# One product for q, k and v, statistics of two tiles per instruction, and new orders of the work in an attention and FFN block

## The chip, the cores and the metric

The kernel runs on one core of a Trainium2 chip. The metric is the device time of one execution in microseconds (us), the median over several runs; lower is better.

## What is computed

The input x has 8 batches of 512 rows of 128 numbers, f32. The output is x + attention(xn) + ffn(xn), where xn is x normalised over its 128 numbers.

```python
qkv = xn @ w_qkv.T                        # 3 x 16 heads x 8
q = softmax((q . code) * scale) * scale   # 2 codes per head
k = (k . code) * scale
k_exp = exp(k - max(k over the 512 rows))
kv = cumsum(k_exp * v) / (cumsum(k_exp) + 1e-9)      # over the rows
xo = sum over codes of q * kv;  attention = xo @ w_out.T
# fp4(): blocks of 16 numbers, scaled by their maximum, rounded to an 8-value grid
h = silu(fp4(xn) @ fp4(w_gate).T) * (fp4(xn) @ fp4(w_up).T)  # 352 wide
ffn = fp4(h) @ fp4(w_down).T
```

## The kernel before, in words

All work is f32 on tiles of 128 partitions; a partition holds 4 neighbouring rows of a batch, so a batch is 4 tiles of 128x128. The weights are quantised and transposed once, at the start. The 8 batches then pass through a software pipeline: each engine runs a loop over steps, and in each step it meets a list of pieces, each for its own batch `b = step - n`. So the text order of the pieces and their `n` are the order of each engine's queue, written out by hand; the last batch has pieces of its own (`if step == ...`). Engines wait for each other on semaphores only. Pieces such as L1416 or L1481 are two throw-away products each on TensorE (30 pieces), placed in gaps of the start.

Per batch the pieces are, in the order of the data:

- Statistics: VectorE `bn_stats` per tile (4 instructions a batch, L893, L961 and others) and `bn_aggr` per tile (4, L1061, L1023 and others); ScalarE takes variance + eps and the negative mean from them; rstd and shift are made on GpSimd (GpSimd = POOL in the rows). Batches 2 and 3, and 4 to 7, share those small steps.
- `xn` on ScalarE (4 activations, L696), transposed on TensorE into the PSUM bank `t_ps` (L1757), copied out by ScalarE to `xn_t` (L794).
- v: 4 products with `wv_t` (128 columns each) into the whole bank `t_ps` (L1458), copied out to `v_sb` (L556). q and k codes: 4 products with `wqk_t` (64 columns each) into half of the bank `a_ps` (L1591). `wqk_t` is w_q and w_k times block-diagonal code matrices `code_bd`, which VectorE builds at the start (L1147, L1148).
- ScalarE takes relu of the q codes (`q_rel`, L674). VectorE takes the maximum of the k codes over the tiles (L1162), TensorE transposes it (L1692), VectorE reduces it (L1234), TensorE subtracts it in the bank (L1729, "kshift"), and ScalarE takes exp into `kv` (L786, "kexp"). Exp/ln and silu lie in two tables of ScalarE, so each batch has two table loads (L784, L629).
- GpSimd multiplies v by exp(k), one operation per code (L500, two a batch), and adds the tiles up (L337, L391, L436). TensorE sums over the partitions into `a_ps` (L1450, "base"), VectorE adds that to all (L992), sums and inverts the denominators with ScalarE's Ln and Exp (L1002, L607, L609, L1038, L1048) and makes `q_n` (L1051); GpSimd makes `o_codes` (L375); TensorE transposes and adds these into `t_ps` (L1660, L1661), and ScalarE copies out (`o_t`, L714).
- Quantising: VectorE maxima, GpSimd scalings `yx`, `xq`, `yh`, `hq` (L495, L430, L449, L516, L399, L461), ScalarE squares into the bank `s_ps`, VectorE two operations each for the grid. `xq` is transposed through `t_ps` as well (L1508, L587).
- FFN: 8 products of 352 columns (L1570, L1571, L1574, L1603, L1654, L1675, L1685, L1711), 4 silus, then 12 transposes of `hq` through `h_ps`, and 16 products for `w_out` and `w_down` into `o_ps` (L1410/L1412, L1499/L1501, L1538/L1540, L1624/L1626). VectorE adds x (L1187), SyncE stores.

A f32 product appears as two records ("x8" for four products), a transpose as one.

Of the kernel before, what the change touches and what calls it, by code (L numbers as in the profile page):

```python
# [4 lines left out]
P = 128  # L5
BATCHES, T, D = 8, 512, 128
TILES = T // P
# [4 lines left out]
FF = 352  # L12
# [19 lines left out]
DEPTH = 89  # L32


# [4 lines left out]
def block_kernel(nc, x, w_qkv, w_out_t, code_t, w_gate, w_up, w_down, out):  # L39
# [6 lines left out]
    with ExitStack() as ctx:  # L46
# [15 lines left out]
        wqk_t = sb("wqk_t", [P, 2 * HC])  # L62
        wv_t = sb("wv_t", [P, D])
# [16 lines left out]
        stats = sb("stats", [P, BATCHES, TILES, 6])  # L80
        meanvar = sb("meanvar", [P, BATCHES, TILES, 2])
# [49 lines left out]
        t_ps = bank("t_ps")  # L131
        h_ps = bank("h_ps")
        a_ps = bank("a_ps")
# [17 lines left out]
        wqkev_done = sem("wqkev_done")  # L151
# [12 lines left out]
        aggr_done = sem("aggr_done")  # L164
# [13 lines left out]
        qk_done = sem("qk_done")  # L178
        qrel_done = sem("qrel_done")
# [5 lines left out]
        v_done = sem("v_done")  # L185
# [8 lines left out]
        qsum_done = sem("qsum_done")  # L194
# [16 lines left out]
        qx_done = sem("qx_done")  # L211
        xqT_done = sem("xqT_done")
        xqt_done = sem("xqt_done")
        gate0_done = sem("gate0_done")
        silu0_done = sem("silu0_done")
        h0_done = sem("h0_done")
# [10 lines left out]
        up3_done = sem("up3_done")  # L227
# [12 lines left out]
        yhz1_done = sem("yhz1_done")  # L240
# [3 lines left out]
        hrz3_done = sem("hrz3_done")  # L244
        hqz3_done = sem("hqz3_done")
# [29 lines left out]
        pads_done = sem("pads_done")  # L275
# [19 lines left out]
        def kv_pairs(p):  # L295
            return kv[:, p, :, :].rearrange("p (a two) r -> p a two r", two=2)

# [30 lines left out]
        def _(pool):  # L328
            nc.gpsimd.memset(ident[:, :], 0.0)
            nc.gpsimd.memset(before[:, :], 1.0)  # L330
            nc.gpsimd.memset(head_of[:, :], 1.0).then_inc(filled, 1)
            for step in range(BATCHES + DEPTH):
                b = step - 52
# [4 lines left out]
                if step == 63:  # L338
                    b = BATCHES - 1
                    p = b % 2  # L340
                    pool.wait_ge(qn_done, 8)
                    nc.gpsimd.tensor_tensor(o_codes[:, p, :, :].rearrange("p j (c w) -> p j c w", w=HEAD), kv[:, p, :, 0:KV].rearrange("p j (c w) -> p j c w", w=HEAD),
                                            q_n[:, p, :, :].unsqueeze(3).broadcast_to([P, TILES, HC, HEAD]), ALU.mult).then_inc(o_done, 1)
                if step == 53:
                    nc.gpsimd.tensor_tensor(ratio[:, 4:8, :], var_eps[:, 4:8, :], guess_sq[:, 4:8, :], ALU.mult).then_inc(ratio_done, 1)
                if step == 30:
                    pool.wait_ge(fills_done, 1)
                    pool.wait_ge(vareps_done, 1)
                    nc.gpsimd.tensor_tensor(rstd[:, 0:1, :], var_eps[:, 0:1, :], minus_half[:, 0:1, :], ALU.pow).then_inc(rstd_done, 1)
                if step == 59:  # L350
                    b = BATCHES - 1
                    p = b % 2
                    pool.wait_ge(kvm_done, 8)
                    nc.gpsimd.tensor_tensor(kv[:, p, 1, :], kv[:, p, 1, :], kv[:, p, 0, :], ALU.add).then_inc(add1_done, 1)
# [1436 lines left out]
```

## Time and profile before

| | |
|---|---|
| median of 3 runs | 145.97 us (145.90 to 146.12) |
| the profiled execution | 145.66 us |
| span of its trace | 143.9 us |
| outside the span | 1.76 us |
| busy: PE, DVE, ACT, POOL | 135.2, 126.0, 115.2, 120.9 us |
| granted TensorE clock | 1.000 of full speed throughout |

PE is TensorE's products, PEld its weight loads, DVE is VectorE, ACT ScalarE, POOL GpSimd. The busy time is the time in which at least one record of the engine runs; the mean durations of records overlap a little, so what an instruction takes in its engine's queue is the distance of two starts.

### The profile page before, as it was taken

To read this page: it belongs to the slowest core of one execution; us is meant where nothing else is said; L and a number is where in the kernel's file an instruction comes from. 1 tells how busy PE (TensorE), PEld (TensorE's weight loads), DVE (VectorE), ACT (ScalarE), POOL (GpSimd) and SP (SyncE) were. 2 spreads that over 40 slices of the span, in tenths; PEclk is the share of its full clock that TensorE was granted. 3 is DMA by queue.
4 is the path that set the end of the run, shared out by engine and by line. 5 is a ranking of instruction groups with operands and counts; after the bars stand their busy time and mean duration, and the time that the engine had idled before them with its cause. 6 is when DMAs were issued, how large, how long until landed. Compare 5 with 4: busy or idle time off the path is not lost.

```text
span 143.9 us, 2675 instructions
## 1 busy us (share of the span) xinstructions
PE 135.2 (94%) x909; PEld 112.8 (78%) x909; DVE 126.0 (88%) x340; ACT 115.2 (80%) x276; POOL 120.9 (84%) x130
## 2 busy tenths in 40 slices
PE   3979999999999999999999999999999998969793
PEld 3979987598869886988698869887988685839692
DVE  0899998999899899989998999899989995999841
ACT  0376788799999989998999899989995797597450
POOL 4567688579999999999889998999599999969920
DMA  4990000000000001000100010001000200010012
GB/s 115 344 343 9 2 0 2 0 0 7 0 0 0 0 5 73 0 0 2 73 5 0 2 73 0 5 0 73 0 0 0 77 0 0 27 48 5 0 73 73
DMA packets 4078, 5.16 MB, mean 36 GB/s; under 512 B 545, under 2 KB 2145, under 8 KB 4065
## 3 DMA queue, kind: packets, MB, share of 16 engines
q1 hardware_dynamic: 3088, 4.49, 8.9%
q10 hardware_dynamic: 976, 0.51, 1.2%
q8 instruction: 7, 0.11, 0.3%
q14 instruction: 7, 0.05, 0.1%
HBM read 2.90 MB, written 2.10 MB: 35 GB/s over the span
## 4 chain that ended last, share of the span: by engine, by line
PE 75%; DVE 11%; ACT 5%; POOL 3%; DMA 2%; issue 1%
PE t_ps L1458 5%; PE a_ps L1591 4%; PE a_ps L1450 3%; PE g_ps L1603 3%; PE u_ps L1570 3%; PE g_ps L1711 3%; PE t_ps L1757 3%; PE u_ps L1574 3%; PE g_ps L1571 3%; PE o_ps L1412 3%; PE u_ps L1654 2%; PE g_ps L1675 2%; PE u_ps L1685 2%; PE o_ps L1626 2%; PE o_ps L1540 2%; PE o_ps L1501 2%
## 5 line engine op out<-in xcount | busy, mean ns | idle before, releaser
L500 POOL TENSOR_TENSOR kv<-v_sb,kv 128x512 f32<-128x512 f32 x14 | 14.8, 1077 | 0.0
L375 POOL TENSOR_TENSOR o_codes<-kv,q_n 128x1024 f32<-128x1024 f32 x7 | 13.8, 1965 | 0.1
L461 POOL TENSOR_TENSOR hq<-qh,h_max 128x704 f32<-128x704 bf16 x7 | 9.7, 1383 | 3.4 <-DVE qh L1307 3.4
L696 ACT ACTIVATE xn<-x_all,shift,rstd 128x128 f32<-128x128 f32 x28 | 11.5, 481 | 0.0
L449 POOL TENSOR_TENSOR yh<-h,h_r 128x704 f32<-128x704 f32 x7 | 9.7, 1386 | 1.5 <-ACT h_r L727 1.5
L399 POOL TENSOR_TENSOR hq<-qh,h_max 128x704 f32<-128x704 bf16 x7 | 9.7, 1386 | 0.0
L516 POOL TENSOR_TENSOR yh<-h,h_r 128x704 f32<-128x704 f32 x7 | 9.7, 1384 | 0.0
L495 POOL TENSOR_TENSOR yx<-xn,x_r 128x512 f32<-128x512 f32 x7 | 7.4, 1058 | 2.6 <-ACT x_r L811 2.6
L992 DVE TENSOR_TENSOR kv<-kv,a_ps 128x1152 f32<-128x1152 f32 x7 | 9.4, 1344 | 0.0
L629 ACT ACT_TABLE_LOAD x7 | 9.0, 1283 | 0.1
L1591 PEld LDWEIGHTS a_ps<-wqk_t,xn_t 128*128 128x128 f32 x56 | 7.3, 191 | 1.3
L784 ACT ACT_TABLE_LOAD x6 | 7.7, 1283 | 0.1
L1458 PEld LDWEIGHTS t_ps<-wv_t,xn_t 128*128 128x128 f32 x56 | 6.9, 191 | 1.0 <-ACT xn_t L794 0.8
L430 POOL TENSOR_TENSOR xq<-qx,x_max 128x512 f32<-128x512 bf16 x7 | 7.4, 1058 | 0.2 <-DVE qx L1093 0.2
L1458 PE MATMUL t_ps<-wv_t,xn_t 128*128 128x128 f32 x56 | 7.6, 278 | 0.0
L1591 PE MATMUL a_ps<-wqk_t,xn_t 128*128 128x64 f32 x56 | 7.0, 268 | 0.0
L1660 PE MATMUL t_ps<-ident,o_codes 128*128 128x128 f32 x28 | 6.5, 273 | 0.0
L1661 PE MATMUL t_ps<-ident,o_codes 128*128 128x128 f32 x28 | 6.5, 272 | 0.0
L1192 DVE TENSOR_REDUCE h_max<-h 128x44 f32<-128x748 f32 x7 | 6.5, 922 | 0.0
L921 DVE TENSOR_REDUCE h_max<-h 128x44 f32<-128x748 f32 x7 | 6.2, 884 | 0.1
L1626 PE MATMUL o_ps<-wd_t,hq_t 128*128 128x128 f32 x42 | 5.8, 275 | 0.0
L1540 PE MATMUL o_ps<-wd_t,hq_t 128*128 128x128 f32 x42 | 5.8, 275 | 0.0
(404 smaller groups left out, 512.7 us busy)
## 6 DMA issues: line engine op xcount, KB each, us to landing
x_all<-x SPq DMA_DIRECT2D x8, 256.0 KB, 4.4
out<-out_sb SPq DMA_DIRECT2D x7, 256.0 KB, 2.0
out<-out_sb SPq DMA_DIRECT2D x2, 128.0 KB, 1.7
w_raw<-w_down ACTq DMA_DIRECT2D x1, 176.0 KB, 4.6
wqk_raw<-w_qkv ACTq DMA_DIRECT2D x1, 128.0 KB, 3.6
w_raw<-w_gate SPq DMA_DIRECT2D x1, 128.0 KB, 3.2
w_raw<-w_up ACTq DMA_DIRECT2D x1, 128.0 KB, 3.5
wv_t<-w_qkv ACTq DMA_DIRECT2D x1, 64.0 KB, 4.4
```

The lines of the kernel that those rows point to most:

```text
L375: nc.gpsimd.tensor_tensor(o_codes[:, p, :, :].rearrange("p j (c w) -> p j c w", w=HEAD), kv[:, p, :, 0:KV].rearrange("p j (c w) -> p j c w ...
L399: nc.gpsimd.tensor_tensor(hq[:, 4 * p + 0:4 * p + 2, 0:FF].rearrange("p t (b k) -> p t b k", k=BLOCK), qh[:, p, 0 * FF:2 * FF].rearrange(" ...
L449: nc.gpsimd.tensor_tensor(blocks(yh[:, p, 0 * FF:2 * FF], PAIR * HB), h[:, p, 0 * HB:2 * HB, 0:BLOCK], spread(h_r[:, p, 0 * HB:2 * HB], PA ...
L461: nc.gpsimd.tensor_tensor(hq[:, 4 * p + 2:4 * p + 4, 0:FF].rearrange("p t (b k) -> p t b k", k=BLOCK), qh[:, p, 2 * FF:4 * FF].rearrange(" ...
L500: last = nc.gpsimd.tensor_tensor(heads(kv[:, p, :, c * D:(c + 1) * D]), heads(v_sb[:, p, :].rearrange("p (j d) -> p j d", j=TILES)), widen ...
L516: nc.gpsimd.tensor_tensor(blocks(yh[:, p, 2 * FF:4 * FF], PAIR * HB), h[:, p, 2 * HB:4 * HB, 0:BLOCK], spread(h_r[:, p, 2 * HB:4 * HB], PA ...
L629: nc.scalar.activation(silu[:, 1, :], g_ps[:, 0:FF], ACT.Silu).then_inc(silu1_done, 1)
L696: last = nc.scalar.activation(xn[:, p, j * D:(j + 1) * D], x_all[:, b, j * D:(j + 1) * D], ACT.Identity, bias=shift[:, b, j:j + 1], scale= ...
L992: nc.vector.tensor_tensor(kv[:, p, :, :], kv[:, p, :, :], a_ps[:, 0:ROW].unsqueeze(1).broadcast_to([P, TILES, ROW]), ALU.add).then_inc(bad ...
L1458: last = nc.tensor.matmul(t_ps[:, j * P:(j + 1) * P], xn_t[:, p, j * P:(j + 1) * P], wv_t[:, :], start=True, stop=True)
L1540: last = nc.tensor.matmul(o_ps[:, 2 * P:3 * P], hq_t[:, 2, c * P:(c + 1) * P], wd_t[:, c * P:(c + 1) * P], start=False, stop=(c == CHUNKS ...
L1591: last = nc.tensor.matmul(a_ps[:, 2 * j * HC:2 * (j + 1) * HC], xn_t[:, p, j * P:(j + 1) * P], wqk_t[:, :], start=(j == 0), stop=False, sk ...
```

## The change

The loads stay as they are, except that w_v lands behind the code weights in one tile `wqkv_t` of 64 + 128 = 192 columns. The two banks `a_ps` and `t_ps` become one tensor of two banks; four products of 192 columns put tiles 0 and 1 of q, k and v into the first bank and tiles 2 and 3 into the second.

```diff
-        t_ps = bank("t_ps")
-        a_ps = bank("a_ps")
+        at_ps = ctx.enter_context(nc.psum_tensor("at_ps", [P, 2, 512], f32))
+        a_ps, t_ps = at_ps[:, 0, :], at_ps[:, 1, :]
+        qkv_ps = at_ps[:, :, 0:2 * QKV].rearrange("p a (j c) -> p a j c", j=2)
...
+                    if b >= 2:
+                        pe.wait_ge(qn_done, b - 1)
+                    for j in range(TILES):
+                        last = nc.tensor.matmul(at_ps[:, j // 2, j % 2 * QKV:(j % 2 + 1) * QKV], xn_t[:, p, j * P:(j + 1) * P], wqkv_t[:, :], start=(j % 2 == 0),
+                                                stop=False, skip_group_check=True)
+                    last.then_inc(qkv_done, 1)
```

The readers follow: relu, the copy of v, and exp(k) each read both banks; the maximum of k waits for the copy of v (`vev_done`); its transpose goes into columns 384 to 511 of `t_ps`; the subtraction is two products, one per bank. `o_codes` of batch b may enter `t_ps` only after exp(k) of batch b + 2, and the transposes of xn only after `o_t`:

```diff
+                    pe.wait_ge(hq0_done, b + 1)
+                    for c in range(CHUNKS):
+                        last = nc.tensor.transpose(h_ps[:, c * P:(c + 1) * P], hq[:, 4 * p + 1, c * P:(c + 1) * P], ident[:, :])
+                    last.then_inc(hqT1_done, 1)
+                    if b < 6:
+                        pe.wait_ge(kexp_done, b + 3)
                     for j in range(TILES):
```

Statistics: two tiles, interleaved, per `bn_stats` (which keeps the moments of even and odd elements apart), so that no `bn_aggr` is needed; ScalarE reads the moments:

```diff
-                    for j in range(TILES):
-                        last = nc.vector.bn_stats(stats[:, 0, j, :], x_all[:, 0, j * D:(j + 1) * D])
+                    for a in range(2):
+                        last = nc.vector.bn_stats(stats[:, 0, a, :], x_all[:, 0, a * 2 * D:(a + 1) * 2 * D].rearrange("p (two d) -> p d two", two=2))
...
-                    for j in range(TILES):
-                        last = nc.vector.bn_aggr(meanvar[:, 0, j, :], stats[:, 0, j, :])
...
+                    nc.scalar.activation(pairs(var_eps[:, 0:1, :]), moments[:, 0:1, :, :, 2], ACT.Copy, scale=1.0 / D, bias=LN_EPS).then_inc(vareps_done, 1)
```

The four operations for `code_bd` move from VectorE to ScalarE. On GpSimd, v times exp(k) is one operation of 1,024 elements:

```diff
-                    for c in range(CODE):
-                        last = nc.gpsimd.tensor_tensor(heads(kv[:, p, :, c * D:(c + 1) * D]), heads(v_sb[:, p, :].rearrange("p (j d) -> p j d", j=TILES)),
-                                                       widen(kv[:, p, :, KV + c * HEADS:KV + (c + 1) * HEADS]), ALU.mult)
-                    last.then_inc(kvm_done, 1)
+                    nc.gpsimd.tensor_tensor(kv[:, p, :, 0:KV].rearrange("p j (c h w) -> p j c h w", c=CODE, w=HEAD),
+                                            v_sb[:, p, :].rearrange("p (j h w) -> p j h w", j=TILES, w=HEAD).unsqueeze(2).broadcast_to([P, TILES, CODE, HEADS, HEAD]),
+                                            kv[:, p, :, KV:ROW].rearrange("p j (c h) -> p j c h", c=CODE).unsqueeze(4).broadcast_to([P, TILES, CODE, HEADS, HEAD]), ALU.mult).then_inc(kvm_done, 1)
```

All pieces get new places. In a turn of the steady part, TensorE's new queue is (batch in brackets): down0 (1), gate1 (3), transposes of hq2 (1), up1 (3), q/k/v (4), gate0 (3), up0 (3), hq3 (1), gate2 (3), up3 (3), transpose of the k maximum (4), up2 (3), gate3 (3), kshift (4), down2 (1), down3 (1), hq1 (2), o_codes (2), base (3), hq0 (2), transposes of xn (5), down1 (2), transposes of xq (4). There are 30 throw-away pieces as before. At the start, the first xn stands ahead of the weights' scale `w_r` in ScalarE's queue, where it stood behind it. The stores are unchanged.

## Rows read from the trace of the kernel before

**Rows 1.** The page's part on busy time, all engines: us, share of the span.
```profile
PE 135.2 (94%) x909; PEld 112.8 (78%) x909; DVE 126.0 (88%) x340; ACT 115.2 (80%) x276; POOL 120.9 (84%) x130
```

**Rows 2.** Windows by stage, all engines: busy us of each engine, clock, DMA.
```profile
core 0: us, PE busy (x) PEld busy (x) DVE busy (x) ACT busy (x) POOL busy (x), PEclk, DMA share, GB/s
...
8.30:24.80 16.50, 15.41 (x118) 13.82 (x117) 15.96 (x70) 13.24 (x37) 12.66 (x16) 1.00 0.15 54
24.80:43.40 18.60, 18.49 (x117) 14.43 (x117) 17.04 (x47) 17.20 (x43) 16.10 (x17) 1.00 0.01 1
43.41:101.43 58.02, 58.02 (x390) 47.92 (x390) 54.66 (x125) 53.81 (x126) 55.24 (x52) 1.00 0.05 19
101.43:115.80 14.37, 14.35 (x95) 11.59 (x95) 13.51 (x31) 11.85 (x28) 13.51 (x12) 1.00 0.05 19
115.80:136.98 21.18, 18.65 (x126) 14.93 (x125) 18.66 (x45) 15.68 (x38) 19.19 (x19) 1.00 0.04 14
```

**Rows 3.** The chain of waits, 57.9 to 72.4 us: start, us, what.
```profile
58.58 0.68 PE a_ps L1450 x2
59.26 0.90 PE t_ps L1458 x8
...
63.62 0.59 PE g_ps L1571 x2
...
64.81 0.84 PE a_ps L1591 x8
```

**Rows 4.** The chain of waits over the whole span, one more piece of it.
```profile
30.76 0.49 PE a_ps L1450 x2
```

**Rows 5.** Windows by turn, the turn of rows 3: columns as in rows 2.
```profile
57.91:72.42 14.51, 14.51 (x100) 11.97 (x99) 13.67 (x32) 13.42 (x32) 13.72 (x13) 1.00 0.05 19
```

**Rows 6.** Timeline of VectorE, end of the denominators in the same turn.
```profile
64.01 0.29 DVE L1051 SCALAR_TENSOR_TENSOR q_n<-a_ps,den_r 128x128 f32<-128x128 f32 x1
```

**Rows 7.** Timeline of VectorE in the start: start us, us.
```profile
5.87 0.16 DVE L1147 TENSOR_SCALAR code_bd<-head_of,code_diff 128x16 f32<-128x16 f32 x1
...
6.29 0.94 DVE L1158 TENSOR_REDUCE w_abs<-w_raw 128x48 f32<-128x768 f32 x1
...
18.20 0.80 DVE L961 BATCH_NORM_STATS2 stats<-x_all 128x6 f32<-128x128 f32 x4
18.93 0.52 DVE L995 SCALAR_TENSOR_TENSOR w_s<-u_ps,w_y 128x352 f32<-128x352 f32 x1
...
20.57 0.37 DVE L1023 BATCH_NORM_AGGREGATE meanvar<-stats 128x2 f32<-128x6 f32 x4
20.85 0.66 DVE L1034 SCALAR_TENSOR_TENSOR sx<-s_ps,yx 128x512 f32<-128x512 f32 x1
```

**Rows 8.** Timeline of ScalarE in the start: start us, us, idle before.
```profile
8.04 0.24 ACT L636 ACTIVATE w_r<-w_recip 128x48 f32<-128x48 f32 x1 [2.23 <-DVE w_recip L957]
8.19 1.63 ACT L696 ACTIVATE xn<-x_all,shift,rstd 128x128 f32<-128x128 f32 x4
```

**Rows 9.** Groups by form on POOL: busy us, mean ns of one.
```profile
L500 POOL TENSOR_TENSOR kv<-v_sb,kv 128x512 f32<-128x512 f32 x14 | 14.8, 1077 | 0.0
L375 POOL TENSOR_TENSOR o_codes<-kv,q_n 128x1024 f32<-128x1024 f32 x7 | 13.8, 1965 | 0.1
```

**Rows 10.** Waits from 43.41 to 101.43 us (four turns): us, times, longest.
```profile
POOL hq L461 <- DVE qh L1307: 2.8, 4, 0.8
DVE den_p L1038 <- ACT a_ps L609: 1.5, 4, 0.4
```

**Rows 11.** Timeline of ScalarE up to exp(k) in a turn.
```profile
67.10 1.63 ACT L696 ACTIVATE xn<-x_all,shift,rstd 128x128 f32<-128x128 f32 x4
...
71.39 1.28 ACT L784 ACT_TABLE_LOAD   x1
72.68 0.28 ACT L786 ACTIVATE kv<-a_ps 128x128 f32<-128x128 f32 x1
```

More of the change, by code:

```diff
@@ new lines, in _ @@
+                if step == 20:
+                    pe.wait_ge(codebd_done, 1)
+                    for s in range(2):
+                        last = nc.tensor.matmul(a_ps[:, s * HC:(s + 1) * HC], wqk_raw[:, s, :],
+                                                code_bd[:, s, :, :].rearrange("p c h -> p (c h)"), start=True, stop=True)
+                    last.then_inc(wqk_done, 1)
+                if step == 33:
+                    for _ in range(2):
+                        nc.tensor.matmul(o_ps[:, 0:P], ident[:, :], before[:, :], start=True, stop=True)
@@ new lines, in _ @@
+                if step == 41:
+                    b = BATCHES - 1
+                    p = b % 2
+                    pe.wait_ge(o_done, 8)
+                    for j in range(TILES):
+                        nc.tensor.matmul(t_ps[:, j * P:(j + 1) * P], o_codes[:, p, j, 0:D], ident[:, :], is_transpose=True, start=True, stop=False)
+                        last = nc.tensor.matmul(t_ps[:, j * P:(j + 1) * P], o_codes[:, p, j, D:KV], ident[:, :], is_transpose=True, start=False, stop=True)
+                    last.then_inc(oT_done, 1)
@@ new lines, in _ @@
+                if step == 33:
+                    for _ in range(2):
+                        nc.tensor.matmul(o_ps[:, 0:P], ident[:, :], before[:, :], start=True, stop=True)
+                if step == 39:
+                    b = BATCHES - 1
+                    p = b % 2
+                    pe.wait_ge(ot_done, 6)
+                    for j in range(TILES):
+                        last = nc.tensor.transpose(t_ps[:, j * P:(j + 1) * P], xq[:, p, j * P:(j + 1) * P], ident[:, :])
+                    last.then_inc(xqT_done, 1)
@@ new lines, in _ @@
+                if step == 32:
+                    pe.wait_ge(wev_done, 1)
+                    for c in range(CHUNKS):
+                        last = nc.tensor.transpose(h_ps[:, c * P:(c + 1) * P], w_dq[:, FFP + c * P:FFP + (c + 1) * P], ident[:, :])
+                    last.then_inc(wT_done, 1)
+                if step == 1:
+                    for _ in range(2):
+                        nc.tensor.matmul(o_ps[:, 0:P], ident[:, :], before[:, :], start=True, stop=True)
+                b = step - 34
```

2164 lines of the change are left out of this document (1042 added, 1122 removed).

## The prediction

> **What bounds the kernel now.** I read the busy times first: all four engines stand between 80% and 94% of the span [rows 1], so no single one is the answer and the stages have to be parted. The windows by stage [rows 2] show three. From 43.41 to 101.43 us the pipeline is in its steady part: four turns of one batch each, PE busy without a gap (58.02 of 58.02), DVE 54.66, POOL 55.24, ACT 53.81. One turn takes 14.51 us [rows 5], and in the chain of waits that turn is TensorE from end to end; only rows of TensorE stand there [rows 3]. So the steady part goes by the length of TensorE's queue, but DVE has 13.67 us and POOL 13.72 us of work in the same turn [rows 5]: 0.84 and 0.79 us below it. From 8.3 to 24.8 us DVE is busy 15.96 of 16.50 us, and then 17.04 of 18.60 us [rows 2]; TensorE's time there is filled with the throw-away products, so the start is VectorE's. From 115.8 us on the last batch drains through short waits between all engines (DVE 18.66, POOL 19.19 of 21.18 us [rows 2]).
>
> The profiled execution took 145.66 us, a span of 143.9 us and 1.76 us around it; the median is 145.97 us. I make the sum against 145.66 and add 0.31 us at the end.
>
> **TensorE in a turn.** Removed are the four v products, 0.90 us, and the four q/k products, 0.84 us [rows 3]. Each product is two records, so a record of 128 columns takes 0.90/8 = 0.112 us and one of 64 columns 0.84/8 = 0.105 us: half the columns save nothing, a record that short costs about as much as one of 128. That is why one product for all three pays. A long record goes by its columns: 352 of them take 0.59/2 = 0.295 us [rows 3], 0.84 ns each. Added are 8 records of 192 columns, 8 x 192 x 0.84 ns = 1.29 us. So 1.74 us become 1.29 us: 0.45 us less. The bounds: 0.84 us less (the records cost what those of v alone cost) and nothing (they cost the sum of both). I take 0.45, since 192 lies between two measured widths, 128 and 352. Kshift becomes two products of 64 columns instead of one of 128; by the q/k record, 4 x 0.105 = 0.42 us, as now, nothing. TensorE also stands still inside its present turn: the base product takes 0.68 us [rows 3] and took 0.49 us where nothing held it [rows 4]. I leave such stalls as large as they are. The granted clock is 1.00, the 2.4 GHz level, in every stage [rows 2], and no idle time is added to TensorE that is longer than those it has, so the clock gets no term. The turn becomes 14.51 - 0.45 = 14.06 us.
>
> Is there room for it? DVE's 13.67 us do not change in a turn (the same 25-odd operations; the maximum of k over the new pattern is the same 128 numbers a partition), and 0.39 us remain above it. Laid end to end with the durations of the rows, the new orders meet each of the new waits narrowly. Exp(k) stands behind the four xn activations (1.63 us), a silu and the table load (1.28 us), 5.9 us from the first xn to its end [rows 11], and the transposes of `o_codes` now wait for it: down2, down3 and the hq1 transposes lie between, and TensorE comes there within 0.2 us of it. `q_n` must be ready before the next q/k/v product: between base and that product lie two groups of transposes of hq, those of xn and xq, two down products, gate1 and up1, about 4.5 us of TensorE. The way from base's end, 59.26 us [rows 3], to the end of `q_n`, 64.30 us [rows 6], is 5.0 us now, with a grid operation in it (0.5 us) that the new order puts later: 4.5 us. That is all the cover there is. Five turns lie between 43.4 and 115.8 us, each with one of the products: 5 x 0.45 = 2.3 us.
>
> **VectorE in the start.** Four `bn_stats` of one tile take 18.93 - 18.20 = 0.73 us of the queue, four `bn_aggr` 20.85 - 20.57 = 0.28 us [rows 7]. There are 8 of each group of four: 5.8 and 2.2 us. The new statistics are 2 instructions of 256 numbers: a `bn_stats` of 128 takes 0.18 us, and the operations of 768 and of 352 numbers, 0.94 and 0.52 us [rows 7], differ by 1.0 ns a number, so 0.13 us are added, so 2 x 0.31 = 0.62 us a batch, 5.0 us in all: 0.8 us less (bounds: nothing, if an instruction of two tiles costs two of one, and 1.5 us). The aggregates go wholly, 2.2 us. The four `code_bd` operations took from 5.87 to 6.29 us, 0.4 us [rows 7]; they go to ScalarE, which waited 2.23 us there [rows 8], so they cost nothing new; if that wait is gone, they cost 4 x 0.15 us before the first xn. Together 3.4 us of DVE, all of it before 31 us. The first xn also leaves the place behind `w_r`, which waited for VectorE until 8.04 us [rows 8]: it can start some 1.5 us sooner, but the weights' path behind it does not get shorter, so I count nothing for it and keep 1.0 us for the range. DVE stood idle 0.54 and 1.56 us in these stages [rows 2], so not all of the 3.4 us reaches the end: I take 2.8 us. Bounds: 1.5 us (the aggregates alone, less those idle times' share) and 4.3 us (everything and the earlier xn).
>
> The Trainium skill, page "SBUF — State Buffer", in the note on cachelines, says that neighbouring reads should fall into one line of 16 bytes and that each step to a new line costs; reading two tiles in turn steps 512 bytes every time. No row here shows a strided SBUF read on DVE, so this rule becomes a rival below.
>
> **POOL.** Two operations of 512 numbers take 2 x 1,077 = 2,154 ns, and an operation of 1,024 numbers with a repeated operand takes 1,965 ns [rows 9]: 0.19 us less per batch (bounds: nothing, and 0.22). It is hidden in a turn, since POOL waits 2.8/4 = 0.7 us in each [rows 10]; in the tail one of them stands on the path: 0.2 us. The page "GPSIMD Engine Reference", section 2.1, of the same skill gives about 2.5 cycles an element as the floor of an operation with two inputs; at its 1.2 GHz that is an estimate of 2.1 us for 1,024 numbers and no gain. The row's 1,965 ns is below that floor, and I go by the row.
>
> **The sum.** 145.66 - 2.8 (start) - 2.3 (five turns) - 0.2 (tail) = 140.4 us, + 0.3 us to the median: **140.7 us**.
>
> **The rivals.**
> - *The turn does not shorten.* TensorE gives up 0.45 us, but the turn then goes by the waits between DVE and ACT: DVE works 13.67 us and waited 0.84 us [rows 5], 1.5/4 = 0.4 us of it for Exp of the denominators [rows 10]. If the waits stay, the turn stays 14.5 us. Only start and tail remain: 145.97 - 3.0 = 143.0 us. Against it: the new order puts two other DVE operations between the logarithm and that wait. Chance 0.2.
> - *Strided statistics.* If each number of a two-tile `bn_stats` costs twice as much, 16 x 256 x 1.0 ns = 4.1 us come back and the start gains nothing: 145.97 - 2.5 = 143.5 us. The skill's cacheline rule would do this. Chance 0.07.
> - *The shared banks stall every turn: slower.* q, k and v now hold both banks from the product to exp(k); before, `o_codes` had `t_ps` without waiting for it. Place: the `o_codes` transposes behind exp(k), and through them the transposes of xn and xq, the gates and the next product. If exp(k) comes 1.6 us after TensorE instead of 0.2, a turn takes 14.06 + 1.4 = 15.5 us, over six turns (one in the late start) 6 x 1.0 = 6.0 us more, less 3.0 us: 145.97 + 3.0 = 149.0 us. It decides from a turn of about 15.0 us (6 x 0.5 = 3.0 us eat the start's gain). For it: three engines are within 0.9 us of the turn, and ACT's queue in front of exp(k) is 5.9 us long. Chance 0.1.
> - *More.* The new orders also take TensorE's stalls (the base product's 0.19 us and as much elsewhere): the turn comes down to 13.7 us and the start gives 4.0 us: 145.97 - 4.0 - 4.0 - 0.2 = 137.8 us. DVE's 13.67 us forbid less. Chance 0.12.
> - *The change doesn't do what it says*: the product of 192 columns costs what the two did and the orders lose what the statistics win, 145.9 us. Chance 0.03.
>
> **How the numbers follow.** My forecast (turn 13.9 to 14.2 us, start 2.0 to 3.5 us: 139.5 to 142.0 us) has a chance of 0.45; 0.03 is left for an unnamed loss. 0.2% is 0.3 us, about what a measurement of this kernel can tell. Faster: 0.45 + 0.2 + 0.07 + 0.12 + 0.01 = 0.85. Same: 0.03. Slower: 0.12. The range leaves out the slower rival (0.1), no change (0.03) and the lower half of "more": 138.0 to 144.0 us.
>
> **What the profile after would show.** Right: one group of 64 records of 192 columns (8 batches) near 1.3 us per four products; a turn of 14.0 to 14.1 us with TensorE still in the chain; 16 `bn_stats` of about 0.32 us and no aggregate; DVE busy about 122.5 us; the first down product 2 to 3 us before 43.4. Wrong: a wait of TensorE for exp(k) or `o_t` above 0.5 us in each turn, DVE busy all through a turn of 14.5 us, or statistics above 0.5 us each.

## The result

The changed kernel takes 144.27 us (median of 6 runs, 143.07 to 145.09) against 145.94 us (145.58 to 146.12) of the kernel before in the same runs: ratio 0.9879, 95% interval 0.9849 to 0.9909. It is faster, by 1.7 us, where 5.3 us were forecast. Measured again it took 144.03 us (143.00 to 145.19) against 145.73 us, ratio 0.986 (0.9826 to 0.9895). Ratios and intervals, here and below, leave out executions more than 1.5% above the fastest of the same kernel, while the medians are of all, so that the two need not agree to the last digit.

The twelve times fall in two groups of six, 143.0 to 143.6 and 144.5 to 145.2 us; the kernel before has one group. The first profile, of an execution of 145.09 us, belongs to the upper group, the second one, of 143.25 us, to the lower. The spans of the twelve are 141.2 to 141.9 us in the lower group; in the upper one four are 143.2 to 143.5 us, one is 142.7 us, and one is 141.9 us, no longer than those of the lower group: there 2.65 us lie outside the span, where the others have 1.7 to 2.1. The page's busy times of the first, against [rows 1]:

```profile
PE 135.0 (94%) x861; PEld 111.1 (77%) x861; DVE 123.5 (86%) x288; ACT 114.6 (80%) x280; POOL 120.0 (84%) x122
```

DVE is down by 2.5 us and by 52 instructions, TensorE by 48 records but only 0.2 us. The turn, in the windows view, against [rows 5]:

```profile
core 0: us, PE busy (x) PEld busy (x) DVE busy (x) ACT busy (x) POOL busy (x), PEclk, DMA share, GB/s
62.11:76.55 14.44, 14.44 (x94) 11.64 (x92) 13.83 (x32) 13.27 (x32) 13.67 (x12) 1.00 0.05 18
```

14.44 us instead of 14.51, where 14.06 were forecast, and TensorE is still busy through all of it. The chain of waits through that turn is again TensorE's from end to end (start, us, what); the rows answer to [rows 3] and [rows 4]:

```profile
62.11 1.30 PE at_ps L1363 x8
63.41 0.81 PE g_ps L1393 x2
...
67.04 0.59 PE g_ps L1466 x2
67.63 0.58 PE at_ps L1482 x4
68.21 0.42 PE o_ps L1514 x2
...
71.39 0.49 PE at_ps L1575 x2
...
72.21 0.53 PE at_ps L1596 x4
```

The same chain in the kernel before, around kshift (L1729), with the pieces beside it:

```profile
70.27 0.59 PE g_ps L1711 x2
70.87 0.41 PE a_ps L1729 x2
71.28 0.59 PE t_ps L1757 x4
...
73.09 0.67 PE a_ps L1450 x2
```

The new product (L1363) is as forecast: 1.30 us for what took 1.74. The base product (L1575) lost its stall as well, 0.49 for 0.68. Both together are 0.63 us, and they are spent again in the same queue. Kshift (L1482) takes 0.58 us for 0.41. The piece behind it (L1514, two records, 0.22 us elsewhere in the turn) takes 0.42, an excess of 0.20; before, the four transposes behind kshift took 0.59 instead of 0.44, an excess of 0.15. Gate0 (L1393) takes 0.81, and the four gates together 2.64 instead of 2.42. The transposes of xn, away from kshift now, still take 0.53 and not 0.44. Back come 0.17 + 0.05 + 0.22 + 0.09 = 0.53 us, and 0.63 - 0.53 leaves the 0.07 to 0.10 us that the turn gained.

For the start I follow one operation that both kernels have, the transposes of xq, for batches 0, 2 and 6, in TensorE's timeline (start us, us). Before:

```profile
19.97 0.61 PE L1508 MATMUL t_ps<-ident,xq 128*128 128x128 f32 x4
...
46.70 0.60 PE L1508 MATMUL t_ps<-ident,xq 128*128 128x128 f32 x4
...
104.72 0.60 PE L1508 MATMUL t_ps<-ident,xq 128*128 128x128 f32 x4
```

After, in the second profile (the first one has all of it 0.3 us later):

```profile
17.98 0.66 PE L1693 MATMUL at_ps<-ident,xq 128*128 128x128 f32 x4
...
44.29 0.61 PE L1693 MATMUL at_ps<-ident,xq 128*128 128x128 f32 x4
...
102.05 0.61 PE L1693 MATMUL at_ps<-ident,xq 128*128 128x128 f32 x4
```

Batch 0 is 2.0 us ahead, batch 2 2.4 us, batch 6 2.7 us: four turns brought the last 0.3. VectorE's last add starts at 138.79 us instead of 141.47, 2.7 us ahead; the tail added nothing. That is the whole gain of the lower group. In the first profile that add starts at 139.09 us, 2.4 us ahead, but the span is only 0.5 us shorter (143.4 for 143.9), because the last store lands later. The DMA view of 139.3 to 143 us in the first profile, with the last store alone, then of 138 to 143 us in the second, with the last two:

```profile
q8 instruction: 1, 0.02, 1.5%
...
out<-out_sb SPq DMA_DIRECT2D x1, 128.0 KB, 3.5
```

```profile
q1 hardware_dynamic: 288, 0.26, 15.0%
...
issues: line engine op xcount, KB each, median us to landing
out<-out_sb SPq DMA_DIRECT2D x2, 128.0 KB, 1.7
```

In the first a packet of 0.02 MB of instruction code (q8) starts at 140.8 us, beside the last store, which lands 3.5 us after its issue; the store before it has landed by then, after 1.7 us. In the second profile the packet does not come, and both land after 1.7 us. These 1.8 us are the difference of the two profiles, apart from the 0.3 us of the start.

### The profile page after: what moved, and what is told of

Its sections match the earlier page's. It is cut to its first block, busy times and chain, and to the rows that moved or that the text cites. A ratio compares the mean times of both kernels' runs of the same rounds, so it can differ in the third digit from the quotient of the medians.

```text
span 143.4 us, 2543 instructions
## 1 busy us (share of the span) xinstructions
PE 135.0 (94%) x861; PEld 111.1 (77%) x861; DVE 123.5 (86%) x288; ACT 114.6 (80%) x280; POOL 120.0 (84%) x122
## 4 chain that ended last, share of the span: by engine, by line
PE 83%; ACT 5%; DVE 4%; DMA 3%; POOL 1%; SPq 1%; issue 1%; ACTq 0%
PE at_ps L1363 6%; PE g_ps L1393 4%; PE o_ps L1528 3%; PE o_ps L1516 3%; PE o_ps L1333 3%; PE o_ps L1665 3%; PE g_ps L1434 3%; PE u_ps L1464 3%; PE u_ps L1407 3%; PE g_ps L1466 3%; PE u_ps L1452 3%; PE g_ps L1339 3%; PE at_ps L1482 3%; DMA w_raw<-w_up 3%; PE u_ps L1352 2%; PE at_ps L1566 2%
## 5 line engine op out<-in xcount | busy, mean ns | idle before, releaser
L358 POOL TENSOR_TENSOR kv<-v_sb,kv 128x1024 f32<-128x1024 f32 x7 | 13.8, 1972 | 0.0
L1363 PEld LDWEIGHTS at_ps<-wqkv_t,xn_t 128*128 128x128 f32 x56 | 9.1, 190 | 2.4 <-DVE q_n L982 1.5
L1363 PE MATMUL at_ps<-wqkv_t,xn_t 128*128 128x192 f32 x56 | 10.5, 330 | 0.5 <-ACT xn_t L674 0.5
L1271 DVE TENSOR_TENSOR kv<-kv,at_ps 128x1152 f32<-128x1152 f32 x7 | 9.4, 1344 | 0.0
L1566 PE MATMUL at_ps<-ident,o_codes 128*128 128x128 f32 x28 | 6.5, 274 | 0.0
L1567 PE MATMUL at_ps<-ident,o_codes 128*128 128x128 f32 x28 | 6.5, 272 | 0.0
L631 ACT ACTIVATE o_t<-at_ps 128x512 f32<-128x512 f32 x7 | 4.2, 598 | 2.4 <-PE at_ps L1567 2.4
L372 POOL TENSOR_TENSOR kv<-kv 128x288 f32<-128x288 f32 x7 | 5.6, 796 | 0.5
L1339 PE MATMUL g_ps<-wg_t,xq_t 128*128 128x352 f32 x14 | 5.7, 489 | 0.2 <-ACT xq_t L722 0.2
L1393 PE MATMUL g_ps<-wg_t,xq_t 128*128 128x352 f32 x14 | 5.9, 500 | 0.1
```

The lines of the kernel that those rows point to most:

```text
L358: nc.gpsimd.tensor_tensor(kv[:, p, :, 0:KV].rearrange("p j (c h w) -> p j c h w", c=CODE, w=HEAD), v_sb[:, p, :].rearrange("p (j h w) -> p ...
L1271: nc.vector.tensor_tensor(kv[:, p, :, :], kv[:, p, :, :], a_ps[:, 0:ROW].unsqueeze(1).broadcast_to([P, TILES, ROW]), ALU.add).then_inc(bad ...
L1339: nc.tensor.matmul(g_ps[:, 0:FF], xq_t[:, p, 1 * P:2 * P], wg_t[:, :], start=True, stop=True).then_inc(gate1_done, 1)
L1363: last = nc.tensor.matmul(at_ps[:, j // 2, j % 2 * QKV:(j % 2 + 1) * QKV], xn_t[:, p, j * P:(j + 1) * P], wqkv_t[:, :], start=(j % 2 == 0) ...
L1393: nc.tensor.matmul(g_ps[:, 0:FF], xq_t[:, p, 0 * P:1 * P], wg_t[:, :], start=True, stop=True).then_inc(gate0_done, 1)
L1566: nc.tensor.matmul(t_ps[:, j * P:(j + 1) * P], o_codes[:, p, j, 0:D], ident[:, :], is_transpose=True, start=True, stop=False)
```

## The experiments

Turns below are a quarter of the way from the xq transposes of batch 2 to those of batch 6. "xq 0" and "xq 2" are the starts of those of batches 0 and 2, "last add" is the start of VectorE's last add, all in us in one profiled execution; the time is the median of the runs and the ratio is against the kernel before, measured along with it. The changed kernel's order was profiled seven times (with e5, e6, e8, e10 and e13, which leave the order of the pieces as it is); those differ by 0.9 us in xq 0 (17.86 to 18.77 us) and in xq 2 (44.18 to 45.08 us). The first maximum over the weights waits for their transfer there and starts between 5.53 and 6.85 us, which is a part of it and not all: at 6.09 and 6.13 us xq 0 came at 17.98 and 18.59. So differences below 0.9 us in the start say nothing, and larger ones are known to within that.

| kernel | xq 0 | xq 2 | turn | last add | time | ratio (95%) |
|---|---|---|---|---|---|---|
| before | 19.97 | 46.70 | 14.51 | 141.47 | 145.73 | 1 |
| after, second profile | 17.98 | 44.29 | 14.44 | 138.79 | 144.03 | 0.986 (0.9826 to 0.9895) |
| e1, product split | 18.68 | 45.64 | 14.70 | 141.62 | 146.03 | 1.0008 (0.9994 to 1.0022) |
| e2, kshift of 128 rows | 18.09 | 44.35 | 14.20 | 137.92 | 142.64 | 0.9755 (0.9728 to 0.9781) |
| e3, up0 ahead of gate0 | 18.09 | 45.25 | 14.70 | 141.25 | 145.79 | 0.9993 (0.997 to 1.0015) |
| e4, aggregates back | 19.57 | 46.22 | 14.44 | 140.71 | 146.18 | 1.0011 (0.9981 to 1.004) |
| e5, POOL in two | 18.74 | 45.05 | 14.43 | 139.53 | 143.60 | 0.9846 (0.9816 to 0.9875) |
| e6, wide fillers | 18.25 | 44.52 | 14.44 | 139.01 | 143.34 | 0.9817 (0.9787 to 0.9847) |
| e7 = e2 + e6 | 18.04 | 44.30 | 14.20 | 137.88 | 142.32 | 0.9757 (0.9719 to 0.9795) |
| e9, before + 128 rows | 19.80 | 46.49 | 14.51 | 141.27 | 145.74 | 0.9996 (0.9981 to 1.001) |
| e11, before + statistics | 19.61 | 46.34 | 14.51 | 141.10 | 145.68 | 0.9985 (0.9966 to 1.0004) |
| e12 = e1 + e4 | 21.14 | 48.29 | 14.70 | 144.25 | 148.01 | 1.014 (1.0104 to 1.0177) |
| e14, before, fillers out | 21.46 | 50.06 | 14.51 | 144.84 | 149.92 | 1.027 (1.0216 to 1.0324) |
| e15 = e14 + statistics | 20.22 | 50.05 | 14.51 | 144.81 | 149.88 | 1.0287 (1.0235 to 1.0338) |
| e16 = e2, fillers out | 19.78 | 46.04 | 14.20 | 139.62 | 144.23 | 0.9793 (0.9714 to 0.9872) |

**The kernel once more**, for a second profile.

> The changed kernel unaltered, for a profile of another execution. If its two groups of times (143.1 to 143.6 and 144.9 to 145.1 us) differ by the landing of the last store, a profiled execution of the quicker group shows the last VectorE add near 139.4 us as before, and a span that ends about 2.1 us after it instead of 4.0 us. If they differ in the turn itself, its six turns add up to about 1.6 us less than 6 x 14.44. Times: 143.0 to 145.1 us.

The landing differs as expected (1.7 us for 3.5), and the turn does not: 14.44 us in both.

**e1: the product split again.**

```diff
-                        last = nc.tensor.matmul(at_ps[:, j // 2, j % 2 * QKV:(j % 2 + 1) * QKV], xn_t[:, p, j * P:(j + 1) * P], wqkv_t[:, :], start=(j % 2 == 0),
+                        nc.tensor.matmul(at_ps[:, j // 2, j % 2 * QKV:j % 2 * QKV + 2 * HC], xn_t[:, p, j * P:(j + 1) * P], wqkv_t[:, 0:2 * HC], start=(j % 2 == 0),
+                                         stop=False, skip_group_check=True)
+                        last = nc.tensor.matmul(at_ps[:, j // 2, j % 2 * QKV + 2 * HC:(j % 2 + 1) * QKV], xn_t[:, p, j * P:(j + 1) * P], wqkv_t[:, 2 * HC:QKV], start=False,
                                                 stop=False, skip_group_check=True)
```

> The one product for q, k and v is issued as two again (64 and 128 columns), eight matmuls a batch instead of four, everything else as changed. Theory A (TensorE's queue bounds the turn, and the 0.45 us that the product gives is spent again at other places of the same queue): turn 14.44 + 0.45 = 14.9 us, time about +0.45 x 6 to 8 = 2.7 to 3.6 us. Theory B (the turn is held by VectorE's and ScalarE's waits, so that TensorE's time is slack): turn 14.4 to 14.5 us, time within 0.5 us of the changed kernel.

Neither size was right. The turn grew by 0.26 us and the time by 2.0 us. In the chain of its turn the eight pieces of the product take 4 x (0.17 + 0.28) = 1.80 us for 1.30, and gate0 takes 0.59 us, where it took 0.81 behind the one product: nearly half of what the product saves is handed to the wait behind it. The other part of the time lies in the start, 1.35 us by batch 2, of which 0.7 us is there at xq 0, within what executions differ by.

**e2: kshift of 128 rows.** Rows 32 to 127 of the stationary side are zeros.

```diff
-        k_negmax = sb("k_negmax", [HC, 1])
+        k_negmax = sb("k_negmax", [P, 1])
...
+            nc.gpsimd.memset(k_negmax[:, :], 0.0)
...
-                        last = nc.tensor.matmul(qkv_ps[:, a, :, HC:2 * HC], k_negmax[:, 0:1].broadcast_to([HC, P]),
-                                                ident[0:HC, 0:HC].unsqueeze(1).broadcast_to([HC, 2, HC]), start=False, stop=True, skip_group_check=True)
+                        last = nc.tensor.matmul(qkv_ps[:, a, :, HC:2 * HC], k_negmax[:, 0:1].broadcast_to([P, P]),
+                                                ident[:, 0:HC].unsqueeze(1).broadcast_to([P, 2, HC]), start=False, stop=True, skip_group_check=True)
```

> The two products that shift the keys by their maximum take 128 rows (rows 32 to 127 are zeros) instead of 32, everything else as changed. Theory A1 (a product of 32 rows is slow by itself, 0.145 us per record, and the first product of 128 rows after it pays about 0.2 us): the four records 0.58 -> about 0.27 us, the two records behind them 0.42 -> 0.22 us, turn 14.44 -> about 13.95 us, time -3 us. Rival (these places wait for VectorE's maximum and for the buffer, whatever the rows): turn stays at 14.4 us, time the same within 0.4 us.

TensorE's timeline around kshift, the changed kernel (first profile), then e2:

```profile
66.87 0.75 PE L1466 MATMUL g_ps<-wg_t,xq_t 128*128 128x352 f32 x2
67.56 0.65 PE L1482 MATMUL at_ps<-ident,k_negmax 32*128 32x64 f32 x4
68.14 0.49 PE L1514 MATMUL o_ps<-wo_t,o_t 128*128 128x128 f32 x2
68.47 0.83 PE L1516 MATMUL o_ps<-wd_t,hq_t 128*128 128x128 f32 x6
```

```profile
66.41 0.76 PE L1467 MATMUL g_ps<-wg_t,xq_t 128*128 128x352 f32 x2
67.01 0.55 PE L1483 MATMUL at_ps<-ident,k_negmax 128*128 128x64 f32 x4
67.40 0.44 PE L1515 MATMUL o_ps<-wo_t,o_t 128*128 128x128 f32 x2
67.67 0.83 PE L1517 MATMUL o_ps<-wd_t,hq_t 128*128 128x128 f32 x6
```

From start to start, gate3, kshift and the next piece take 0.69 + 0.58 + 0.33 = 1.60 us with 32 rows and 0.60 + 0.39 + 0.27 = 1.26 us with 128. So 0.34 us a turn was the price of the 32 rows, of which 0.19 lies in the products themselves and 0.15 in the changes before and behind them; no wait for VectorE's maximum is in it, since e2 has the same wait and TensorE goes on without it. Theory A1 had the cause, and was too high in size: the turn is 14.20 us and not 13.95. The Trainium skill, page "TensorE: Matmul & The Clock Gate", section "Why this matters for your kernels", has a single product of 32 rows cost the same time as one of 128. These rows, of f32 and 64 columns, do not agree: 0.145 us a record with 32 rows, 0.098 with 128. The turn shortened by 0.24 us, not by 0.34, for its chain now runs through other engines:

```profile
73.62 0.45 DVE sh L1288
...
74.09 0.54 DVE qh L1298
...
74.70 0.60 ACT s_ps L754
...
75.32 1.28 ACT L768
...
76.62 0.47 ACT silu L768
...
77.13 0.86 PE g_ps L1394 x2
```

VectorE's grid operation, ScalarE's square, the table load (1.28 us) and silu1 now release gate0. In that turn of 14.22 us TensorE is busy 14.16, DVE 13.66, POOL 13.65 and ACT 13.17 us. In the last add e2 is 0.87 us ahead of the changed kernel; the median falls by 1.4 us, since two of its six times and not three lie in an upper group (143.8 us here).

**e3: up0 ahead of gate0**, to cover that wait.

```diff
+                    nc.tensor.matmul(u_ps[0][:, 0:FF], xq_t[:, p, 0 * P:1 * P], wu_t[:, :], start=True, stop=True).then_inc(up0_done, 1)
                     pe.wait_ge(silu1_done, b + 1)
                     nc.tensor.matmul(g_ps[:, 0:FF], xq_t[:, p, 0 * P:1 * P], wg_t[:, :], start=True, stop=True).then_inc(gate0_done, 1)
...
-                    nc.tensor.matmul(u_ps[0][:, 0:FF], xq_t[:, p, 0 * P:1 * P], wu_t[:, :], start=True, stop=True).then_inc(up0_done, 1)
```

> TensorE issues up0 ahead of gate0, which waits for ScalarE's silu1, everything else as changed. If the 0.23 us that gate0 takes more than before the change is that wait, and TensorE's queue is the bound: gate0 0.82 -> 0.6 us, turn 14.44 -> about 14.2 us, time -1.2 to -1.6 us. If the turn is held elsewhere (silu0 comes 0.3 us later and the whole feed-forward chain with it): turn 14.4 to 14.7 us, time the same or up to 1.5 us longer.

The second case, with 145.79 us a little above its range. Gate0 goes down to 0.59 us, but gate2, behind the hq3 transposes, now waits: in TensorE's timeline of e3

```profile
65.36 0.49 PE L1422 MATMUL h_ps<-ident,hq 128*128 128x128 f32 x3
66.07 0.86 PE L1434 MATMUL g_ps<-wg_t,xq_t 128*128 128x352 f32 x2 [0.23 <-ACT silu L818]
```

0.71 us from the one to the other, 0.33 before. The turn is 0.26 us longer. My reading, which no further run tests: the wait belongs to ScalarE's path from the table load on, and taking gate0 later only lengthens that path.

**e4: the old statistics.** Each batch again has four `bn_stats` of one tile and, right behind them, four `bn_aggr`.

> The statistics as before (four bn_stats of 128 columns and four aggregates a batch, 32 of each), everything else as changed: some 3.1 us more of VectorE in the first 30 us. Theory S1 (VectorE bounds the start, as the prediction had it): nearly all of it arrives, the query transposes of batch 2 and all behind them 2.4 to 2.8 us later, time +2.4 to +2.8 us. Theory S2 (the start is TensorE's queue and its waits for ScalarE, and VectorE has idle stretches there now): +0.3 to +1.3 us.

1.9 us by batch 2 and in the last add, between the two forecasts, a little nearer to S1. In eight of its twelve executions the mean granted clock was below 1 (0.998 once, 0.988 six times, 0.977 once); the four at 1.000, the profiled one among them, took 145.29 to 146.15 us. So a part of the median's 2.15 us is the clock's (see e12). The aggregates stand right behind the statistics here, for batch 1 ahead of the reciprocal of the weights' maxima, on which the quantising waits; elsewhere they might cost less.

**e5: v times exp(k) as two operations on POOL.**

> v times exp(k) as two GpSimd operations again (2 x 1.08 instead of 1.97 us a batch), everything else as changed. Prediction: 0.19 us a batch, off the chain that bounds, about 0.2 us at the end. If the base product's stall on GpSimd's additions (0.67 us a turn before, 0.49 us now) is what this operation removed, the turn grows by up to 0.19 us and the time by 1.0 to 1.3 us.

Nothing that can be told: the turn is the same, and the last add is 0.74 us later, within what executions differ by; the weights landed 0.76 us later in this one (the maximum over them starts at 6.85 us, for 6.09). The operation itself takes 1.97 us, as forecast, and wins under 0.2 us that nobody waits for.

**e6 and e7: wide fillers.** Each pair of throw-away products of 128 columns becomes one of 256, 120 instructions fewer for TensorE.

```diff
-                    for _ in range(2):
-                        nc.tensor.matmul(o_ps[:, 0:P], ident[:, :], before[:, :], start=True, stop=True)
+                    nc.tensor.matmul(o_ps[:, 0:2 * P], ident[:, :], before[:, :].unsqueeze(1).broadcast_to([P, 2, P]), start=True, stop=True)
```

> Each of TensorE's 30 pairs of filler matmuls of 128 columns is one matmul of 256 columns: the same columns, 120 fewer instructions in TensorE's stream, everything else as changed. Theory F (the slow group of times comes from an instruction fetch of 16 KB, queue q8, that falls into the last stores at 139 to 141 us): the seventh fetch is no longer reached, all executions land their last store in 1.7 us and the times lie together at 143.0 to 143.6 us. Rival (the landing is slow by chance): two groups as before, a third to half of the times at 144.5 to 145.2 us.

> The wide fillers together with the key shift of 128 rows. If the two effects are separate: turn 14.2 us, no slow last store, all times together at 141.6 to 142.2 us, against 142.6 us (141.7 to 143.8) with the 128 rows alone.

In e6 the seventh code packet is gone, and five of six times lie at 143.05 to 143.38 us; one is 145.26, with a mean clock of 0.988 and a span of 143.5 us, so that a late time does not need the packet. The five fit, and prove little: e5, whose TensorE program is that of the changed kernel, had no late group either (143.39 to 144.22 us). e7 has the 128-row shift besides, 142.32 us in the median, four of six times at 141.90 to 142.39 us; one is 145.92, with a mean clock of 0.976. Its last add is 1.13 us ahead of e6's. It and e2 are the fastest kernels of this study, 3.1 to 3.5 us below the one before.

**e8, e10 and e13: the code packet moved.** 24, 12 and 5 more instructions stand in TensorE's stream while it is idle at the start (48, 24 and 10 waits; two of them make one instruction).

```diff
+                    for _ in range(48):
+                        pe.wait_ge(filled, 1)
                     pe.wait_ge(consts_done, 1)
```

> 24 more instructions in TensorE's stream, before its first product (waits on a semaphore that is already set, while the engine has nothing to do), everything else as changed. By the fetches of 16 KB seen every 20 us of TensorE's stream, the seventh comes some 2 us earlier than the 140.75 us where one profile had it, near 138.8 us. Theory F (the slow group is the last store beside that fetch): the fetch now falls into the last stores in every execution, all times at 144.5 to 145.2 us, stores landing in 2.6 us in the median. Rival (chance, or the waits themselves): times in two groups as before, or all longer by the same with the last VectorE add later.

> 12 more instructions in TensorE's stream before its first product (24 more brought the seventh fetch from 140.75 to 136.81 us, ahead of the last stores): the fetch should come at 138.6 to 139.2 us, where the kernel with the 128-row shift had it and was slow. Theory F: most executions at 144.5 to 145.2 us, in the profile the fetch between 138 and 141 us and the last stores landing in about 2.6 us. Rival (fetch and landing have nothing to do with each other): a profile with the fetch there and landings of 1.7 us.

> 5 more instructions in TensorE's stream before its first product (12 more brought the seventh fetch to 137.91 us, 1.1 us ahead of the first of the last stores; none left it at 140.75 us or out): the fetch should come between 138.9 and 140.3 us, within the flight of the last stores. Theory F: landing about 2.6 us in the median and times at 144.5 to 145.2 us in most executions. Rival: landing 1.7 us with the fetch there.

All three missed: the packet came at 136.9 us, at 138.1 us and not at all, each time outside the flight of the last stores, which landed after 1.7 us. Times: 143.81 (143.15 to 144.74), 143.97 (143.51 to 145.55) and 143.70 us (142.85 to 145.66). All three kernels have executions above 144.5 us all the same. Whether the packet makes the upper group of times was not shown this way. What the profiles do show is below, under the hardware.

**e9: the kernel before with 128 rows in kshift**, the same edit on L1729.

> The kernel before, with its single key-shift product taking 128 rows (96 of them zeros) instead of 32. If a product of 32 rows costs by itself and makes the next one slower, here too: L1729's two records 0.41 -> 0.3 us, the transposes behind them 0.50 -> 0.44 us, turn 14.50 -> 14.35 us, time -0.9 to -1.1 us against the kernel before. If the gain of the other experiment came from something of the changed kernel alone: the same within 0.2%.

The first half came true, the second did not. Kshift takes 0.22 us from start to start for 0.41, with the pieces around it 0.35 us less, and the turn stays at 14.51 us. The chain of waits in e9 says why:

```profile
70.06 0.61 PE g_ps L1712 x2
...
70.69 0.47 ACT silu L772
...
71.18 1.28 ACT L785
...
72.47 0.29 ACT kv L787
...
72.80 0.75 PE a_ps L1451 x2
```

From gate3 to base the old turn goes through ScalarE: silu, table load, exp(k), 2.1 us in all. What TensorE does meanwhile (kshift, the xn transposes, an hq group, a down product) has slack. In the profile before this path was hidden: TensorE was held for 0.19 us at base (0.68 us for 0.49 [rows 3, 4]), and the chain gave the time to base.

**e11: the kernel before with the new statistics**, in the old order. The first profile fell in an execution of 480 us and says nothing; the places in the table are from a second one, time and ratio from the first measurement. The second gave 145.80 us and a ratio of 1.0004 (0.9987 to 1.0022).

> The kernel before with the new statistics alone (two bn_stats of 256 columns a batch, no aggregates, the moments read by ScalarE), in the old order: 3.0 us less of VectorE before 31 us. The prediction's step has it that this shortens the start by nearly as much: query transposes of batch 2 some 2.5 us sooner and time -2.3 to -2.8 us. If the start hangs on the landing of the weights and on latencies as the changed kernel's does (its aggregates cost it 1.9 us): -1.5 to -2.0 us. If VectorE's stretch is free: within 0.3 us.

> The kernel before with the new statistics alone once more, for its profile (the first one fell in an execution of 480 us). Its times of 145.3 to 145.9 us leave 0.2 us of gain. If VectorE's 3.0 us are off the chain in the old order, the query transposes of batch 0 come at 19.9 us and of batch 2 at 46.5 us as before, and TensorE or ScalarE's weights' work is what they wait for. If they are won and given back: batch 0 at 18 us and a turn longer than 14.5 us behind it.

The time is the same within 0.3 us, the last case of the first text, and xq 0 and xq 2 fit the first case of the second. Of VectorE's 3 us, 0.36 us reach the old kernel's pipeline, about what the four aggregates of batch 0 took (0.34 us of VectorE's queue). The first xn transposes come 0.36 us sooner (9.52 for 9.88 us), and from there to 31 us TensorE's queue, fillers included, runs as before, only 0.36 us ahead.

**e12: e1 and e4 together.**

> The changed kernel with both the product split in two and the old statistics. If the two effects at the start are separate (product 1.35 us and statistics 1.93 us by the query transposes of batch 2) and a turn costs 0.26 us more: transposes of batch 2 at 44.3 + 3.3 = 47.6 us against 46.70 in the kernel before, last VectorE add near 143.8 us, time 147.8 to 148.3 us, slower than before by about 2 us; then the remade orders and the shift of two products cost about 2 us that the two savings pay back. If one hides the other: transposes of batch 2 at 46.2 to 46.7 us, time 146.2 to 147.2 us.

Xq of batch 2 comes at 48.29 us, beyond the first case. But the clock has a part in that which neither case has. TensorE was idle for 1.95 us before the first product, and soon after it the granted clock fell to 0.50, the 1.2 GHz level, up to 16.9 us; in the windows view (columns as in rows 2):

```profile
10.90:12.90 2.00, 0.06 (x2) 0.01 (x1) 1.93 (x15) 1.67 (x5) 0.88 (x1) 1.00 0.10 40
13.50:16.90 3.40, 3.40 (x18) 3.40 (x18) 2.44 (x5) 1.11 (x5) 2.23 (x3) 0.50 0.01 2
```

Three of its executions, with a mean clock of 1.000 or 0.999, took 147.12 to 147.54 us; the profiled one and another, with 0.988, took 148.49 and 148.77. By these the fall costs some 1.3 us. Less that (my estimate), xq of batch 2 would come at 47.0 us, 0.3 us behind the kernel before, which is within what executions differ by, and the time is 1.5 to 1.9 us above it. That lies between the two cases and decides for neither. What remains shown of the price of the remade orders and the two-product kshift, with both savings undone, is the turn: 0.19 us each, 1.0 us in five.

**e14, e15 and e16: the fillers behind the first xn transposes taken out**, 21 pairs of the old and 19 of the new order.

> The kernel before without the 21 pairs of filler matmuls that stand behind its first transposes of xn (9 pairs ahead of them stay); nothing of the output depends on them. Theory Q (TensorE's queue, fillers included, sets the pace of the start: 11 pairs of 0.45 us lie between the first transposes of xn and the first of xq, where the changed kernel has 7): the first xq transposes well ahead of 19.97 us, by 1.5 to 4 us, and the time 1.5 to 4 us shorter if the clock stays up. Rival (the fillers only fill waits): first xq transposes at 19.5 to 20 us and time within 0.4 us; or the granted clock falls and the start becomes longer.

> The same with the new statistics in the old order as well. If the fillers were what hid VectorE's savings: 1.5 to 2.5 us less than without them alone. If VectorE is off the chain of the start in the old order anyway: 0.2 to 0.4 us less, as with the fillers in place.

> The changed kernel with the 128-row shift and without the 19 pairs of fillers behind its first transposes of xn. Theory Q: against 142.6 us with the 128 rows alone, 1 to 2.5 us less (17 pairs of 0.45 us lie before 41 us, most of them in waits for ScalarE and VectorE). Rival: the same within 0.4 us, or longer if the granted clock falls.

Theory Q failed: without fillers the second xn transposes of e14 come at 16.90 us (16.74 before), so up to there they only fill waits. Then the clock falls; the windows view of e14, and of the kernel before:

```profile
10.00:20.00 10.00, 6.98 (x39) 5.73 (x40) 9.45 (x35) 6.93 (x20) 6.71 (x8) 0.80 0.06 24
20.00:33.00 13.00, 10.84 (x39) 6.43 (x38) 9.53 (x42) 8.56 (x21) 7.67 (x11) 0.76 0.01 2
```

```profile
10.00:20.00 10.00, 10.00 (x86) 9.64 (x87) 9.68 (x36) 7.71 (x22) 6.97 (x8) 1.00 0.06 22
20.00:33.00 13.00, 12.65 (x80) 9.90 (x79) 12.13 (x50) 11.20 (x32) 9.89 (x14) 1.00 0.00 1
```

The granted clock is 0.80 and 0.76 in the mean there: from 16.0 to 26.2 us it is 0.50, the 1.2 GHz level, after TensorE had been busy for 2.66 of the 5.1 us before. The kernel takes 4.2 us more. e15 gains 1.2 us more at batch 0 and has lost it again at batch 2, but its clock also falls 1.3 us later (17.3 us) and stays down as long, so e15 cannot tell whether VectorE's saving would have arrived at a full clock. e16 varies from 142.09 to 147.2 us, with a mean clock of 0.999 to 0.953; its fastest, at 0.999, is no faster than e2's.

## Why the prediction was wrong

The product saved what was forecast, and the turn shortened by 0.07 us instead of 0.45. Two steps of the prediction failed there, the second and the third below.

- *TensorE in a turn, the product.* Right in itself: 1.30 us for 1.29 forecast.
- *"Kshift becomes two products of 64 columns ... 4 x 0.105 = 0.42 us, as now, nothing."* This failed. The records have 32 rows, and I took the price of a record of 128. They cost 0.145 us each, 0.58 in all, and the piece behind them 0.05 us more than before: 0.22 us of the 0.45. The old kshift took 0.41 us for two records, 0.2 a record: that was there to be read, though its records are of 128 columns and these of 64.
- *"I leave such stalls as large as they are."* This failed too. The base stall went (-0.19 us), and the gates (+0.22) and xn transposes (+0.09) took its place. It was no constant but the visible end of a path through ScalarE. A wait adapts: e1 showed that a TensorE piece that is 0.50 us longer costs the turn 0.26 us, e2 that 0.34 us less gives 0.24, e9 that 0.35 us less in the old order gives nothing.
- Together five turns brought 0.3 us instead of 2.3: 2.0 of the 2.6 us by which the lower group misses.
- *VectorE in the start*, 2.8 us: 2.4 us by batch 2, the right size for the wrong reason. Two `bn_stats` of two tiles take 0.61 us of the queue, as forecast (0.62). But in the old order this wins 0.36 us (e11). The gain comes from a new order of the start that uses it, and by e1 1.35 us of it, give or take the 0.9 us that executions differ by, is the product's, which I had counted in the turns only. The fillers, which both kernels have 30 of, were moved as well (11 pairs lie between the first transposes of xn and of xq before, 7 after), and I did not price them. How the 2.4 us divide over these is not settled: e1 gives back 1.35 us and e4 1.9, together 4.0 and, less the clock's part, 2.7, each known to within 0.9 us.
- *POOL*, 0.2 us: nothing that can be told at the end (e5).
- *Stores*: I had no term for the last store. In the first profile it lands 1.8 us late, and half the executions take 1.2 to 1.9 us more than the lower group's 143.3 us. That is the difference between a time inside my range and one outside of it. That the store is the cause is shown for the profiled execution alone; three more have spans that fit, and one, of 141.9 us, cannot have it.

Of the rivals, "the turn does not shorten" came nearest, 143.0 us against 143.3 of the lower group, though TensorE stays in the chain and it was not VectorE's waits that kept the turn. "Strided statistics" fell: a `bn_stats` of 256 strided numbers takes 0.42 us and one of 128 neighbouring ones 0.27. The 0.15 us of difference are 1.2 ns a number, against the 1.0 that I assumed for numbers read in order, so a doubled price is excluded. The slower rival fell: no wait for exp(k) or `o_t` stands in the turn.

## What to carry to other kernels

A chain that lies on one engine from end to end does not prove that the engine's queue is the bound: look at whether a piece takes longer in the chain than elsewhere, and which path of another engine ends there; 0.19 us on one product was the tip of a path with no slack. Price a product by records of its own shape, rows included; where 32 rows stand among 128, padding with zeros is worth a try (here 0.34 us of TensorE's time a turn, and 0.9 to 1.1 us at the last add; in the old order, with its path through ScalarE, nothing). Throw-away products that keep the clock up are part of the order: taking them out cost 4.2 us here. And where a change makes TensorE wait longer in the start, look at the granted clock of every execution before you price it: of the 148.49 us of e12's profiled execution some 1.3 were the clock's.

## What was not expected of the hardware

A store lands late where a packet of instruction code starts soon after its issue. The packets come every 20 us or so (16 KB each, queue q8) and are TensorE's: with 120 instructions fewer in its stream (e6) the first comes at 22.8 us instead of 16.2, and there are six. In the kernel before one comes at 112.5 us, beside the store of batch 4, and in e9 at 111.8; the DMA view of 110.5 to 114 us of the two:

```profile
q8 instruction: 1, 0.02, 1.6%
issues: line engine op xcount, KB each, median us to landing
out<-out_sb SPq DMA_DIRECT2D x1, 256.0 KB, 3.4
```

```profile
q8 instruction: 1, 0.02, 2.1%
issues: line engine op xcount, KB each, median us to landing
out<-out_sb SPq DMA_DIRECT2D x1, 256.0 KB, 3.1
```

Stores of that size land after 2.0 us otherwise. In all, six profiles have stores with a packet that starts 0.2 to 1.4 us after their issue, nine stores (before 2.9 and 3.4 us, after 3.5, e2 3.4, e9 3.1 and 3.1, e11 2.9 and 2.9, e8 2.6), and in the others with their fillers in place no store took over 2.1 us. A packet in the last 0.2 us of a store changes nothing (e2, the store before the last: 1.7 us). In mid-kernel this costs nothing (in the kernel before, the turn from xq 2 on has the store of 2.9 us in it and takes 14.51 us, as the next one does); in the changed kernel and in e2 it was the last store, on which the end waits. That fits the page "DMA: Bandwidth & Descriptors" of the Trainium skill, section "Queues, rings and completion order": a DMA engine takes turns between its queues packet by packet; the rows show the late landing, not the turns themselves. That the upper group of times consists of just these executions is not so for one of the six (span 141.9 us) and unproven for four.
